# Experts 4 to 7 of a merged feed-forward layer: grouped by 32 rows and summed in narrow column groups, in place of one diagonal per expert

## What is computed

```python
gh = relu(x @ gfc1_w.T + gfc1_b)
g = (gh @ gfc2_w.T + gfc2_b).mean(rows)          # 8 numbers, one for each expert
W1m = W1 + sum_e g[e] * tv_W1[e]                 # (F, D) = (256, 512), fp32
b1m = b1 + g @ tv_b1
W2m = W2 + sum_e g[e] * tv_W2[e]                 # (D, F)
b2m = b2 + g @ tv_b2
h = relu(x @ W1m.T + b1m)
out = layernorm(x + h @ W2m.T + b2m)
```

## Time and profile before

| | |
|---|---|
| median of three runs | 511.06 us (510.05 to 512.14) |
| the profiled execution's own time | 510.37 us |
| its span, first to last instruction | 508.6 us |
| mean granted TensorE clock | 0.975 |
| PE busy | 470.0 us (92%) |
| DVE busy | 324.8 us (64%) |
| ACT busy | 250.3 us (49%) |
| POOL busy | 166.1 us (33%) |
| chain that ended last | PE 75%, DVE 14%, ACT 5%, issue 3% |

### The profile page before, as it was taken

One profiled execution on the slowest core, in us unless ns is written; L12 is line 12 of the kernel. 1 busy time (PEld: TensorE's weight loads), 2 busy tenths in 40 slices (PEclk: granted clock), 3 DMA queues, 4 the chain that ended last, 5 costly groups with the idle time before them and its releaser, 6 DMA issues.

```text
span 508.6 us, 9887 instructions
## 1 busy us (share of the span) xinstructions
PE 470.0 (92%) x3564; PEld 358.0 (70%) x3564; DVE 324.8 (64%) x749; ACT 250.3 (49%) x524; POOL 166.1 (33%) x176
## 2 busy tenths in 40 slices
PE   1989999999999998999999997999999879989892
PEld 1768567886765676666999984679998768956641
DVE  4766698747999846754655358634333675439687
ACT  4787354147712354254344755424346477724454
POOL 1369243111095003033326880003323023304403
PEclk9999999999999989999999999999999959989998
DMA  8700102202020002002100001000000394000014
GB/s 241 210 3 18 66 0 85 84 1 84 0 85 0 2 3 84 0 14 79 77 0 0 1 6 57 1 0 1 0 6 0 124 411 210 1 0 2 1 54 148
DMA packets 5246, 27.44 MB, mean 54 GB/s; under 512 B 1036, under 2 KB 1161, under 8 KB 3544
## 3 DMA queue, kind: packets, MB, share of 16 engines
q1 hardware_dynamic: 5208, 26.92, 15.4%
HBM read 24.36 MB, written 2.56 MB: 53 GB/s over the span
## 4 chain that ended last, share of the span: by engine, by line
PE 75%; DVE 14%; ACT 5%; issue 3%; POOL 1%; DMA 1%; SPq 0%; DVEq 0%; ACTq 0%
PE ps L459 46%; PE ps L631 17%; PE ps L448 4%; PE ps L725 3%; PE ps L524 2%; PE ps L534 1%; PE ps L445 1%; DVE r L1665 1%; DVE late L1168 1%; DVE r L1167 1%; DVE r L1677 1%; POOL late L1718 1%; DVE ohs L1158 1%; DVE r L1655 1%; DMA x<-in_x 1%
## 5 line engine op out<-in xcount | busy, mean ns | idle before, releaser
L459 PE MATMUL ps<-r,wslot 128*128 128x250 f16 x840 | 98.1, 277 | 4.4 <-DVE r L1167 4.3
L459 PEld LDWEIGHTS ps<-r,wslot 128*128 128x128 f16 x840 | 83.0, 100 | 16.8 <-DVE r L1167 5.8
L631 PE MATMUL ps<-late,r 125*128 (+1 forms) x800 | 87.1, 269 | 0.9 <-DVE r L1387 0.9
L1726 POOL TENSOR_TENSOR wslot<-stage,wslot 128x512 f16<-128x512 f32 x32 | 39.5, 1266 | 139.6 <-ACT wslot L777 139.6
L631 PEld LDWEIGHTS ps<-late,r 125*128 125x128 f16 x800 | 77.4, 97 | 10.8 <-issue 1.6
L459 PE MATMUL ps<-wslot,r 128*125 128x512 f16 x300 | 69.4, 381 | 0.0
L459 PE MATMUL ps<-wslot,late 128*125 128x512 f16 x240 | 54.9, 380 | 3.1 <-DVE late L1459 2.7
L459 PEld LDWEIGHTS ps<-wslot,r 128*125 128x125 f16 (+1 forms) x300 | 39.3, 136 | 22.4 <-issue 2.3
L1754 POOL TENSOR_TENSOR late<-ohs,late 128x250 f16<-128x250 f32 x40 | 25.6, 651 | 88.8 <-ACT late L953 88.8
L459 PE MATMUL ps<-late,wslot 128*128 (+1 forms) x480 | 51.7, 269 | 0.0
L459 PEld LDWEIGHTS ps<-late,wslot 128*128 128x128 f16 x480 | 46.5, 97 | 5.3 <-issue 0.8
(11 more groups left out here) (183 smaller groups left out, 732.3 us busy)
## 6 DMA issues: line engine op xcount, KB each, us to landing
late<-in_tv SPq DMA_DIRECT2D x2, 4096.0 KB, 17.3
x<-in_x SPq DMA_DIRECT2D x5, 448.0 KB
out<-r SPq DMA_DIRECT2D x10, 224.0 KB
stage<-in_w_up SPq DMA_DIRECT2D x2, 1024.0 KB, 5.5
stage<-in_w_down SPq DMA_DIRECT2D x2, 1024.0 KB, 5.3
stage<-in_w_lin SPq DMA_DIRECT2D x1, 1024.0 KB, 6.4
stage<-in_w_k SPq DMA_DIRECT2D x1, 1024.0 KB, 4.8
stage<-in_w_q SPq DMA_DIRECT2D x1, 1024.0 KB, 4.7
```

The lines of the kernel that those rows point to most:

```text
L459: last = nc.tensor.matmul(out, stat_(hs, b), mov(hm, b), start=start and n == 0, stop=stop and n == 3 * blocks - 1)
L631: last = nc.tensor.matmul(bank("t", m), u_nat[layer][:, p, h, m * 128:(m + 1) * 128], counts(h)[:, chunk], start=(start and h == 0 and p = ...
L1726: last = nc.gpsimd.tensor_tensor(wslot[:, i % SLOTS, 1, k, :], stage[:, k * D:(k + 1) * D], wslot[:, i % SLOTS, 0, k, :], ALU.subtract)
```

## The change

Experts 4 to 7 are loaded in another layout. Partition group e (32 partitions) now holds expert 4+e, and its four slots hold that expert's rows 0 to 31, 32 to 63, 64 to 95 and 96 to 127. This takes one DMA of all 128 partitions for experts 0 to 3 and four DMAs of 32 partitions for experts 4 to 7, for each of the two weight matrices: ten DMAs in place of two.

A single 128x32 matrix `g_stack` replaces the four diagonals: in the row of expert e and row i of its group it has g[e] in column i. It is made on DVE: two reductions of the identity ahead of the gate's wait, and two instructions after gcol, which pick each partition's own g and multiply. ACT's four instructions are gone. One matmul with g_stack on slot j sums all four experts for the rows 32j to 32j+31 and writes the 32 PSUM partitions of group j, so a part takes four matmuls, each with `start` and `stop` set, for four experts. PE now takes four experts in each part (before 4, 3, 4, 3) and DVE four (before 4, 5, 4, 5).

```diff
-PE_SHARE = (4, 3, 4, 3)
+GROUP = 32
+GROUPS = 128 // GROUP
...
             sp.wait_ge(full["t"], before("t", "gate"))
+            whole = E - PE_EXPERTS
+            grouped = dram["tv"].rearrange("(j i) w e n -> i w j e n", j=GROUPS)
             for w in range(2):
-                sp.dma_start(tv[:, w], dram["tv"][:, w]).then_inc(got_tv, 16)
+                sp.dma_start(tv[:, w, 0:whole], dram["tv"][:, w, 0:whole]).then_inc(got_tv, 16)
+                for e in range(PE_EXPERTS):
+                    sp.dma_start(tv[e * GROUP:(e + 1) * GROUP, w, whole:, :], grouped[:, w, :, whole + e, :]).then_inc(got_tv, 16)
...
-            def merge_on_pe(bank_, part, share):
-
-                for k in range(PE_EXPERTS - share, PE_EXPERTS):
-                    pe.wait_ge(diag_ready, k + 1)
-                    last = nc.tensor.matmul(bank_, g_diag[:, k, :], part(E - PE_EXPERTS + k), start=(k == PE_EXPERTS - share),
-                                            stop=(k == PE_EXPERTS - 1))
+            def merge_on_pe(bank_, part):
+
+                pe.wait_ge(diag_ready, 1)
+                for j in range(GROUPS):
+                    last = nc.tensor.matmul(bank_[j * GROUP:(j + 1) * GROUP], g_stack[:, :], part(E - PE_EXPERTS + j),
+                                            start=True, stop=True)
                 last.then_inc(pe_merged, 1)
...
-            pe.wait_ge(got_tv, 32)
+            pe.wait_ge(got_tv, 32 * (1 + PE_EXPERTS))
...
-            act.wait_ge(g_col, 1)
-            for k in range(PE_EXPERTS):
-                e = E - PE_EXPERTS + k
-                nc.scalar.activation(g_diag[:, k, :], ident[:, :], ACT.Copy, scale=gcol[:, e:e + 1]).then_inc(diag_ready, 1)
...
+            then(nc.vector.tensor_reduce(of_group[:, :], ident[:, :].rearrange("p (e i) -> p i e", e=GROUPS), AX.X, ALU.add))
+            then(nc.vector.tensor_reduce(in_group[:, :], ident[:, :].rearrange("p (e i) -> p e i", e=GROUPS), AX.X, ALU.add))
             wait_done(dve, "t", "gate", 20)
...
             dve.wait_ge(g_col, 1)
+            then(nc.vector.scalar_tensor_tensor(g_picked[:, :], gcol[:, E - PE_EXPERTS:], 1.0, in_group[:, :], ALU.mult, ALU.mult,
+                                                accum_out=g_own[:, :]))
+            nc.vector.tensor_scalar(g_stack[:, :], of_group[:, :], g_own[:, 0:1], None, ALU.mult).then_inc(diag_ready, 1)
             dve.wait_ge(got_wm, 16)
-            dve.wait_ge(got_tv, 32)
+            dve.wait_ge(got_tv, 32 * (1 + PE_EXPERTS))
...
-            merge(w1_part(wm32[:, 0, :], 1), lambda e: w1_part(tv[:, 0, e, :], 1), E - PE_SHARE[1])
+            merge(w1_part(wm32[:, 0, :], 1), lambda e: w1_part(tv[:, 0, e, :], 1), E - PE_EXPERTS)
```

More of the change, by code:

```diff
@@ L77 @@
 PE_EXPERTS = 4
-PE_SHARE = (4, 3, 4, 3)
+GROUP = 32
+GROUPS = 128 // GROUP
+assert PE_EXPERTS == GROUPS
 S_B, LOW_ROW = 64.0, 32
@@ L222, in gps_block @@
         tvrow = ohs[0:E, 2 * KB * CH:2 * KB * CH + 6 * D].bitcast(F32).rearrange("e (r c) -> e r c", r=3)
-        g_diag = ohs[:, 2 * KB * CH + 6 * D:2 * KB * CH + 6 * D + PE_EXPERTS * 256].bitcast(F32).rearrange(
-            "p (e n) -> p e n", e=PE_EXPERTS)
+        g_stack = ohs[:, 2 * KB * CH + 6 * D:2 * KB * CH + 6 * D + 2 * GROUP].bitcast(F32)
+        of_group, in_group = (ohs[:, 2 * KB * CH + 6 * D + a:2 * KB * CH + 6 * D + b].bitcast(F32)
+                              for a, b in ((64, 64 + 2 * GROUP), (128, 128 + 2 * GROUPS)))
+        g_own, g_picked = (ohs[:, 2 * KB * CH + 6 * D + a:2 * KB * CH + 6 * D + a + 2 * n].bitcast(F32)
+                           for a, n in ((144, 1), (152, GROUPS)))
         b2_ones = ohs[0:2 * LOW_ROW, OHS - 128:OHS]
@@ L730, in merge_w1 @@
                 merge_on_pe(ps[:, bank_, :].rearrange("p (k f) -> p k f", k=KB),
-                            lambda e: tv[:, 0, e, :].rearrange("p (k f) -> p k f", k=KB)[:, :, m * 128:(m + 1) * 128], PE_SHARE[m])
+                            lambda e: tv[:, 0, e, :].rearrange("p (k f) -> p k f", k=KB)[:, :, m * 128:(m + 1) * 128])
             def merge_w2(bank_, h):
-                merge_on_pe(ps[:, bank_, :], lambda e: tv[:, 1, e, h * D:(h + 1) * D], PE_SHARE[FB + h])
-            pe.wait_ge(got_tv, 32)
+                merge_on_pe(ps[:, bank_, :], lambda e: tv[:, 1, e, h * D:(h + 1) * D])
+            pe.wait_ge(got_tv, 32 * (1 + PE_EXPERTS))
             wait_done(pe, "y", "gnn", T)
@@ L756, in merged_at @@
         def merged_at(part):
-            return sum(2 * (E - n) + 1 for n in PE_SHARE[:part + 1])
+            return (part + 1) * (2 * (E - PE_EXPERTS) + 1)
         @block.scalar
@@ L1612, in low_w1 @@
                     w1m[:, 0, :, part * 128:(part + 1) * 128], S_W).then_inc(wm_split, 1)
-            merge(w1_part(wm32[:, 0, :], 0), lambda e: w1_part(tv[:, 0, e, :], 0), E - PE_SHARE[0])
+            merge(w1_part(wm32[:, 0, :], 0), lambda e: w1_part(tv[:, 0, e, :], 0), E - PE_EXPERTS)
             wait_full(dve, "x", "g", 1)
@@ L1637, in merge_w2 @@
                 merge(wm32[:, 1, half(h)].rearrange("p (k n) -> p k n", k=2),
-                      lambda e: tv[:, 1, e, half(h)].rearrange("p (k n) -> p k n", k=2), E - PE_SHARE[FB + h])
+                      lambda e: tv[:, 1, e, half(h)].rearrange("p (k n) -> p k n", k=2), E - PE_EXPERTS)
             def low_w2(h):
```

## The result

The changed kernel takes 513.29 us (median of 8 runs, 511.25 to 514.43) against 510.65 for the kernel before in the same comparison: 1.0061 of it, 95% interval 1.0043 to 1.0080. It is slower, by about 0.6%. The forecast was 509.5, faster than before, with a range from 507.0 to 513.2: the sign is wrong, and the measured median lies 0.1 us above the range. The ratios leave out three stray slow executions (608.99 us in e5, 2658.46 in e8, 1210.89 in the kernel before beside them), which the medians given for these runs still count.

The account below looks back on a forecast made before the run. The prediction took PE to bound the kernel from the gate to about 480, with DVE close behind. It summed 2.4 us won less 0.8 for the clock to 1.6 us earlier, forecasting 509.5 us, range 507.0 to 513.2.

Parts of the forecast that it names:

- the clock's term of the sum: Before ffn2: PE's pause of 2.7 us may drop the clock, costing 1.7 us; half taken, 0.8 us.
- What bounds the kernel: Gate to ffn2: PE bounds until about 480 with DVE close behind; after the change DVE bounds from about 460.
- Overlap of narrow matmuls: PE merge: partial overlap, 5 slots (matmul records of 0.43 us at full clock) per part, bounds 2 and 8.
- Start of the merge: After gcol: DVE's two new instructions take 0.50 us (0.4 to 0.7); identity reductions, some 0.2 us each, are covered.
- Loads: Weight loads before the merge: 32-partition pieces at half speed land at 439 and cost nothing.
- The fourth merge beside POOL: DVE's Merge_w2(1), eight instructions partly beside POOL's hidden chunks: 4.2 us, bounds 3.26 and 6.4.
- The sum without the clock: Merge through to ffn2: ffn2 starts at 478.9 instead of 481.29, 2.4 us earlier.
- rival (3): Gate to ffn2: full overlap, but the clock stays low too long; between 511.4 and 513, taken as 512; chance 0.08.
- Rival (1): PE merge: narrow matmuls run one after the other, costing 1.7 us, 512.8; chance 0.22.
- Rival (4): Weight loads: slower than a third of full rate; at a quarter both engines wait 8.9 us, 520; chance 0.05.
- Rival (2): Merge to ffn2: overlap, POOL hardly meets the last merge, clock stays up; gain 3.5 us, 507.5; chance 0.15.
- the middle class: Whole kernel: a time between 508.5 and 513.6 us, given 0.66; faster had 0.24, slower 0.10.

Follow-up runs that it names:

- e5: Changed kernel with all eight experts summed on PE and DVE's 32 merge instructions removed: 507.13 us, 0.9925 of the kernel before.
- e8: Kernel before with ten loads of tv in place of two, old layout: 510.28 us, 0.9995 of the kernel before.
- e2: Changed kernel with unused matmuls: 22 before ffn2, 5 while PE waits for the gate's sums, 10 after merge part 0: 506.81 us, 0.9924 of the kernel before.
- e3: Changed kernel with all four narrow matmuls of a part on one column group: 513.19 us, 1.0056 of the kernel before.
- e6: Kernel before with 5 unused matmuls on PE while it waits for the gate's sums: 508.79 us, 0.9962 of the kernel before.
- e1: Changed kernel with 20 unused matmuls on PE in the pause before ffn2: 510.13 us, 0.9992 of the kernel before.
- e7: Changed kernel run again unaltered for a second profile: 512.02 us, 1.0041 of the kernel before.
- e4: Kernel before with four experts on PE in every part, diagonals kept: 511.82 us, 1.0013 of the kernel before.
- e9: e5 with 5 unused matmuls on PE while it waits for the gate's sums: 501.96 us, 0.9843 of the kernel before.

## Why the prediction was wrong, step by step

The step that failed is the clock's term of the sum. The sum had 2.4 us won by the merges and 0.8 us lost by one possible fall of the clock before ffn2. Measured, the clock's low stretches took 2.2 us near the gate, where the sum had nothing for more low clock than the 3.4 us of before, and 2.4 at ffn2, and turned the gain into a loss. Step by step:

- **What bounds the kernel: right.** PE and DVE were two nearly equal chains, and DVE took over. Its merges stand in the chain now.
- **Overlap of narrow matmuls: wrong in size.** I took 5 slots for a part, arguing that the two records of one matmul would block the next group. Measured: 8 records in 1.06 us at full clock (e2), some 2.5 slots, and 16 in 1.92. Four groups run at once, records or not; e3 shows that it is this and not the narrow weights. The error didn't bring a gain, since DVE was the bound anyway, but made PE's pauses longer: block 1 should have ended 26.1 us after the reduction, and ends after 25.6 in the changed kernel in spite of the low clock, and after some 23.1 in e2.
- **Start of the merge: right.** DVE's first merge stands 1.69 us after the reduction and stood at 1.32: 0.37 later, against 0.50 taken with bounds from 0.4. PE's stands at 1.92 and stood at 1.87. The two reductions of the identity took 0.36 and 0.29 us, more than some 0.2 each, and were covered.
- **Loads: right.** The last was issued by 411.5, where the slowest landing of its line is 28.3 us: 439.8 at the latest, against the 439 taken, and 13 us before its use. The whole took 32.7 us from the first issue, 9.8 more than before, about what half the rate for half of the bytes gives (10.8). The Trainium skill (SBUF — State Buffer, "Door 1: The DMA port swizzle") lets 32 partitions reach 8 of the 16 ports, and the trace agrees with that in size.
- **The fourth merge beside POOL: 4.87 us** and not 4.2, inside its bounds. 0.7 us of the sum.
- **The sum without the clock: nearly right.** 2.4 us earlier at ffn2 was the forecast; e2, whose clock stays up, has its last low half 2.7 us earlier. Part of that is not the merges but a low clock that the kernel before pays for and that is moved off the path: against e6, where it is gone too, 1.0 is left.
- **The clock: the step that failed.** For the front I let PE bring the clock back at 455.9 as before, because with 5 slots it would have been busy until then. With about 2 it was done at 455.86 in spite of the half clock and then stood for 1.5 us, and the clock stayed low for 10.4 us instead of 3.4. This was rival (3) in its mechanism: part 1 at half clock, ffn1's first chunks dear, low_w1(1) waiting for high_w1(1) behind hidden(1). Its sizes were off: it had low_w1(1) 1.0 us later than before, and measured from the reduction it is 0.3 earlier (14.79 against 15.07), though 1.5 later than the forecast's 13.3. The loss came at ffn2. I gave this rival 0.08, because I held full overlap for unlikely, and didn't ask how long the pause would be in the cases between. Whether the pause of 1.5 us alone kept the clock down is not shown: in e3, with no pause behind the start of the merge, the clock was low for 3.4 us, but in e5, with none either, for 6.7. For the back I priced a fall at 1.7 us and took half of it, from the one fall that had lasted 3.4 us. The pause was 5.2 us and not 2.7, the clock was low for 6.8 us, and the cost was 2.35 to 2.5 (e1), 2.8 in e7. The trace of before has a longer fall, near 410, which I had looked at and left out of the bound (stretch, PE to POOL busy, clock):

```profile
408.20:418.40 10.20, 8.31 (x39) 7.18 (x38) 7.92 (x19) 7.23 (x15) 2.50 (x2) 0.50 0.97 416
```

  With 10.2 us at half clock in view, a bound of 1.7 us was too low. And the forecast had a cost for the back alone, where both came.
- **Rival (1)** priced what e3 makes true: 1.7 us, with 2.6 measured. **Rival (4)** is refuted by the landings and by e8. **Rival (2)**, the clock staying up, would have been 3.5 us below the kernel before; e2, with the clock kept up, is 3.8 below. That this is so near is in part luck: the rival also had POOL hardly meet the last merge, which takes 4.87 us in e2 as well.
- **The range.** The chances are split at 508.5 and 513.6, 2.6 us to either side of the kernel before, and not at the ends of the range. By them 513.29 falls in the middle class, to which I gave 0.66; by the range it lies outside.

Put together: 2.7 us won (e2), 2.2 lost near the gate (e2 against the change) and 2.4 at ffn2 (e1) leave a loss of 1.9. These are differences along one path and add up by themselves; the independent check is that each of the two fillings gives its part back. The two profiles of the changed kernel show 1.87 and 2.55 (60.40 and 61.08 against 58.53), the medians 2.6 and 1.5.

## What to carry to other kernels

When an engine whose clock depends on its work is made quicker without the next engine in line, its gain becomes a pause, and the price of the pause has to stand in the sum: bound it by the longest low-clock stretch in the trace, and do so for each pause. Look at the clock column first in any stretch where TensorE waits on a handful of small instructions; matmuls that nobody reads, put into the wait, tell within one run what the clock costs there. And if one engine has time to spare after a change, give it the other's work: that was worth 3.4 us here without fillers and 8.2 with them, where the change alone lost. Set the fillers' own part off: on the kernel before they won 1.7 us. And compare a change at equal clock as well: the 2.7 us that this one seems to win with fillers is 1.0 against a kernel before that has them too.

## What the runs showed of the hardware

- Four fp32 matmuls with 32 output columns each on different column groups: 16 records of 512 columns in 1.85 to 1.92 us at full clock, 32 in 3.57. On one group 8 take 3.55 (e3), and with 128 columns 16 take 6.87 (e4's chain). Hardly any cost of switching between narrow and wide matmuls shows: in e9 part 0, b2 and part 1 follow each other in 1.92, 1.05 and 1.85 us, b2 takes the same 1.05 between wide matmuls in the kernel before, and 16 of the 32 in a row take 1.79.
- TensorE's clock fell to 1.2 GHz after pauses near the gate of 1.3 and 0.5 us with a few small matmuls between, and in full stops of 5.2 us before ffn2; it stayed up over stops of 0.8 and 1.3 us there. Once down near the gate it stayed down for 3.4 us in the kernel before and in e3 and for 6.7 in e5, in all three with PE working on without a break, and for 10.4 and 10.2 in the changed kernel (e7 the second), where PE paused again.
- A DVE merge instruction of 256 fp32 columns takes 0.41 us alone and 0.80 in the third part, beside a busy POOL: 6.40 to 6.42 us for eight in every kernel that has these merges. In the fourth part eight take 3.26 where POOL's work comes later (e3, e4) and 4.87 where it overlaps (the changed kernel, e1, e2).
